# First and last layer of a four-layer graph network: float16 products accumulated in one 256-column half of a bank, four output banks in turn

## The reference

```python
# layer 0
node_att = softmax(x @ node_w, axis=0)
h = x @ edge_w
e = where(adj > 0, h @ h.T, NEG_BIG)
output = adj * (node_att * softmax(e, axis=1)) @ (x @ weight) + bias
# layer 1: gated sum of an attention with rank-one scores and of adj @ (x @ W_gcnb)
# layer 2: relu(normalised (adj + I) @ (x @ weight))
# layer 3
h = relu(adj @ (x @ W1) + b1)
h = relu(adj @ (h @ W2) + b2)
output = adj @ (h @ W3) + b3
# after each layer: x = layernorm(x + output)
```

## Time and profile before

| | |
|---|---|
| median of 3 runs | 790.58 us (789.51 to 792.78) |
| the profiled execution | 791.85 us, its span 790.0 us |
| granted TensorE clock over the span | 0.988 of full speed |
| PE busy | 744.8 us (94%), 4192 matmuls |
| DVE busy | 452.6 us (57%) |
| ACT, POOL busy | 347.4 us, 120.0 us |
| `weighted`, L696 and L698 | 256 and 256 matmuls |
| last product, L953 and L963 | 64 and 192 matmuls |
| layer 0's rounds | about 46 to 213 us of the span |
| last product | 726.8 us to the end |

### The profile page before, as it was taken

One profiled execution on the slowest core, in us unless ns is written; L12 is line 12 of the kernel. 1 busy time (PEld: TensorE's weight loads), 2 busy tenths in 40 slices (PEclk: granted clock), 3 DMA queues, 4 the chain that ended last, 5 costly groups with the idle time before them and its releaser, 6 DMA issues.

```text
span 790.0 us, 11567 instructions
## 1 busy us (share of the span) xinstructions
PE 744.8 (94%) x4192; PEld 489.8 (62%) x4192; DVE 452.6 (57%) x934; ACT 347.4 (44%) x530; POOL 120.0 (15%) x246
## 2 busy tenths in 40 slices
PE   7888999797999999999989999999999999999997
PEld 6776766564678878787835545675664546465343
DVE  4485888688768797988944475121271311114465
ACT  4678877675385474646722243132270322224000
POOL 2011222111321012111122340000001000000343
PEclk9998999998999999999999999999999999999999
DMA  8948889996568509400030000000000000000011
GB/s 230 180 91 146 162 164 159 167 155 112 103 95 153 88 2 159 68 2 1 1 87 1 0 0 1 1 0 0 0 0 27 1 1 0 0 0 0 21 41 46
DMA packets 114300, 48.71 MB, mean 62 GB/s; under 512 B 103504, under 2 KB 109776, under 8 KB 114256
## 3 DMA queue, kind: packets, MB, share of 16 engines
q1 hardware_dynamic: 110224, 33.44, 21.7%
q0 software_dynamic: 4032, 14.68, 11.2%
HBM read 35.53 MB, written 2.10 MB: 48 GB/s over the span
## 4 chain that ended last, share of the span: by engine, by line
PE 43%; DVE 7%; issue 3%; ACT 1%; POOL 1%; DVEq 0%; POOLq 0%; ACTq 0%
PE ps L777 11%; PE ps L928 11%; PE ps L904 8%; PE ps L963 4%; PE ps L937 3%; PE ps L887 3%; PE ps L953 2%; DVE stats L1297 1%; PE ps L633 1%; DVE es_lo L1285 1%; DVE x L1575 1%; DVE tm L1495 1%; DVE agg_lo L1483 1%; DVE y L1619 0%; DVE y L1697 0%
## 5 line engine op out<-in xcount | busy, mean ns | idle before, releaser
L777 PE MATMUL ps<-adjT,x 128*128 128x512 bf16 (+1 forms) x768 | 173.3, 379 | 5.1 <-DVE agg_lo L1483 2.5
L777 PEld LDWEIGHTS ps<-adjT,x 128*128 128x128 f16 x768 | 72.3, 98 | 90.4 <-issue 7.6
L696 PE MATMUL ps<-sup,turned 128*128 128x512 f16 x256 | 88.3, 393 | 12.1 <-DVE y L1350 12.1
L1285 DVE TENSOR_TENSOR hh_lo<-hf,hh_hi 128x512 fp32r<-128x512 f32 x32 | 22.2, 693 | 134.5 <-ACT hf L1221 133.5
L928 PE MATMUL ps<-adjT,G 128*128 x384 | 83.6, 379 | 0.4 <-ACT hf L1221 0.4
L819 PE MATMUL ps<-H_hi,es_hi 128*128 128x258 f32 x256 | 76.8, 300 | 2.2 <-DVE es_lo L1285 1.7
L819 PE MATMUL ps<-H_lo,es_hi 128*128 128x258 f32 x256 | 72.4, 283 | 0.0
L819 PE MATMUL ps<-H_hi,es_lo 128*128 128x258 f32 x256 | 72.4, 283 | 0.0
L698 PE MATMUL ps<-sup,turned 128*128 128x256 f16 x256 | 71.7, 280 | 0.0
L928 PEld LDWEIGHTS ps<-adjT,G 128*128 128x128 f16 x384 | 37.3, 98 | 45.4 <-issue 0.9
L492 POOL TENSOR_TENSOR rstd<-mv,epsc 128x1 f32<-128x1 f32 x64 | 15.2, 238 | 295.9 <-DVE mv L1299 295.9
(11 more groups left out here) (216 smaller groups left out, 1484.7 us busy)
## 6 DMA issues: line engine op xcount, KB each, us to landing
adjb<-in_adj POOLq DMA_DIRECT2D x16, 512.0 KB, 7.0
adjf<-in_adj POOLq DMA_DIRECT2D x12, 512.0 KB, 6.4
x<-in_x SPq DMA_DIRECT2D x4, 512.0 KB, 6.0
out<-adjf SPq DMA_DIRECT2D x16, 128.0 KB, 1.7
adjf<-in_L_gnn_W SPq DMA_DIRECT2D x1, 1024.0 KB, 5.9
W1f<-in_L_gnn_W SPq DMA_DIRECT2D x1, 512.0 KB, 3.7
adjf<-in_L_gnn_W SPq DMA_DIRECT2D x1, 512.0 KB, 3.9
we<-in_L_gnn_edge_w SPq DMA_DIRECT2D x1, 256.0 KB, 3.8
```

What stands on the lines that cost most here:

```text
L696: ins = mm(bank(6 + u), PT(HI, t)[:, jt, :], sup[:, jt, :], start=(jt == 0), stop=False, skip_group_check=True)
L777: ins = mm(bank(4 + f), x16[:, part, jt, f * P:(f + 1) * P], adj(b, jt), start=(jt == 0 and part == HI), stop=(jt == T - 1 and part == LO))
L1285: return tt(to, frm, high.bitcast(F32), ALU.subtract)
```

## The change

Both products now accumulate all their parts in the same 256 columns, in matmuls of 256 columns. In layer 0 three of them (P_hi S_hi, P_hi S_lo, P_lo S_hi) stand where one of 512 and one of 256 stood; in the last product two stand where one of 512 stood. The number of columns streamed is the same; each matmul brings its weight load. DVE reads 256 columns once (L1350 and L1699 are gone, and the semaphore `xb_used` with them). The last product takes banks 0 to 3 in turn, so a tile waits for the read of tile t - 4, and tiles 4 to 7 wait for nothing. DVE's register loop over the last tiles is written out.

```diff
-                    ins = mm(bank(6 + u), PT(HI, t)[:, jt, :], sup[:, jt, :], start=(jt == 0), stop=False,
-                             skip_group_check=True)
-                    ins = mm(bank(6 + u, D), PT(LO, t)[:, jt, :], sup[:, jt, 0:D], start=False, stop=(jt == T - 1),
-                             skip_group_check=True)
+                    for part, c0 in ((HI, 0), (HI, D), (LO, 0)):
+                        ins = mm(bank(6 + u, D), PT(part, t)[:, jt, :], sup[:, jt, c0:c0 + D],
+                                 start=(jt == 0 and (part, c0) == (HI, 0)), stop=(jt == T - 1 and part == LO))
...
-                    ins = mm(bank(4 + k), adjT[:, 0, jt, k * P:(k + 1) * P], f16[:, jt, :], start=(i == 0),
-                             stop=(i == T - 1))
+                    for part in (HI, LO):
+                        ins = mm(bank(4 + k, D), adjT[:, 0, jt, k * P:(k + 1) * P], f16[:, jt, part * D:part * D + D],
+                                 start=(i == 0 and part == HI), stop=(i == T - 1 and part == LO))
...
             def out3(b, k):
-                t, u = TB * b + k, k % 2
-                if not (isinstance(b, int) and k < 2):
-                    pe.wait_ge(o3_read, t - 1)
+
+                if not isinstance(b, int):
+                    pe.wait_ge(o3_read, TB * b + k - TB + 1)
                 for jt in range(T):
-                    ins = mm(bank(u), adjT[:, bass.ds(b, 1), jt, k * P:(k + 1) * P].rearrange("p a c -> p (a c)"),
-                             f16[:, jt, :], start=(jt == 0), stop=(jt == T - 1))
+                    for part in (HI, LO):
+                        ins = mm(bank(k, D), adjT[:, bass.ds(b, 1), jt, k * P:(k + 1) * P].rearrange("p a c -> p (a c)"),
+                                 f16[:, jt, part * D:part * D + D], start=(jt == 0 and part == HI),
+                                 stop=(jt == T - 1 and part == LO))
...
-                stt(y[:, u, :], bank(6 + u, D), rowf[:, u, 2:3], xb[:, u, :], ALU.mult, ALU.add).then_inc(xb_used, 1)
-                dve.wait_ge(xb_used, t + 1)
-                stt(y[:, u, :], ps[:, 6 + u, D:2 * D], rowf[:, u, 2:3], y[:, u, :], ALU.mult, ALU.add) \
-                    .then_inc(pv_read, 1)
+                stt(y[:, u, :], bank(6 + u, D), rowf[:, u, 2:3], xb[:, u, :], ALU.mult, ALU.add).then_inc(pv_read, 1)
...
             def final3(t, u):
-                at = 4 + t if isinstance(t, int) and t < TB else u
+                at = 4 + t if t < TB else t % TB
...
-                stt(y[:, u, :], bank(at, D), g1[:, 3:4], xb[:, u, :], ALU.mult, ALU.add).then_inc(xb_used, 1)
-                dve.wait_ge(xb_used, T + t + 1)
-                stt(y[:, u, :], ps[:, at, D:2 * D], g1[:, 3:4], y[:, u, :], ALU.mult, ALU.add).then_inc(o3_read, 1)
+                stt(y[:, u, :], bank(at, D), g1[:, 3:4], xb[:, u, :], ALU.mult, ALU.add).then_inc(o3_read, 1)
...
-            pair3(1)
-            with dve.Fori(2, T // 2) as i:
-                own.enter(i - 2, 2)
+            for i in range(1, T // 2):
                 pair3(i)
-            own.leave(T // 2 - 2)
```

More of the change, by code:

```diff
@@ L357, in build @@
         PT_landed = [sem(f"PT_landed{part}") for part in (HI, LO)]
-        pv_mm, pv_read, xb_ready, xb_used = sem("pv_mm"), sem("pv_read"), sem("xb_ready"), sem("xb_used")
+        pv_mm, pv_read, xb_ready = sem("pv_mm"), sem("pv_read"), sem("xb_ready")
         y_normed = sem("y_normed")
@@ L494, in norm_factor, with bias_x @@
                     .then_inc(rstd_ready, 1)
-            def bias_x(t, u, before=0):
-                wait_from(pool, xb_used, before + t - 1)
+            def bias_x(t, u, used):
+                wait_from(pool, used, t - 1)
                 nc.gpsimd.tensor_tensor(xb[:, u, :], tile(x, t), brow[:, :], ALU.add).then_inc(xb_ready, 1)
@@ L522, in _ @@
                 load_adj(t)
-            bias_x(0, 0)
-            bias_x(1, 1)
+            bias_x(0, 0, pv_read)
+            bias_x(1, 1, pv_read)
             def load_later(t):
@@ L544, in _ @@
                 if t + 2 < T:
-                    bias_x(t + 2, t % 2)
+                    bias_x(t + 2, t % 2, pv_read)
                 if t + 2 * AB < T:
@@ L610, in _ @@
             nc.gpsimd.partition_all_reduce(g1[:, 1:2], g1[:, 0:1], P, RMAX).then_inc(gmax_ready, 1)
-            bias_x(0, 0, T)
-            bias_x(1, 1, T)
+            bias_x(0, 0, o3_read)
+            bias_x(1, 1, o3_read)
             with pool.Fori(0, T // 2 - 1) as i:
@@ L617, in _ @@
                     norm_factor(3 * T + 2 * i + u, u)
-                    bias_x(2 * i + 2 + u, u, T)
+                    bias_x(2 * i + 2 + u, u, o3_read)
             own.leave(T // 2 - 1)
```

## The result

| | before | changed |
|---|---|---|
| median of 7 runs | 792.78 us | 786.98 us |
| lowest to highest | 789.51 to 794.17 | 783.11 to 806.39 |
| ratio, 95% interval | | 0.9919 (0.9891 to 0.9948) |
| profiled execution: time, span | 791.85, 790.0 | 785.21, 783.4 |

A second measurement of the same two kernels, 12 and 17 runs on another chip (the last experiment), gave 787.99 and 791.14 us, ratio 0.9963 (0.9939 to 0.9987). The kernel is faster by 0.4 to 0.8%; the predicted time of 785.6 was 1.4 us too low by the first median and 2.4 by the second, and the range of 782.5 to 790.5 held both. Two of the first seven runs, at 802 and 806 us, lie far above the others.

The account below looks back on a forecast made before the run. PE bounds the kernel at both ends of layer 0 and in the last product, DVE with near-full DMA queues between. Layer 0's -2.9 and the last product's -2.1 us take 790.58 to 785.6 us; range 782.5 to 790.5.

Parts of the forecast that it names:

- The last product: Last product and tail: wait gone -2.1 us, one read less in the tail -0.52, pace +0.5; sum -2.1 us.
- The pace: Last product: 256-column matmuls start 0.109 us apart, their loads costing nothing; +0.5 us over 256 pairs.
- The two ends of layer 0: Layer 0, 79 to 125 us and from 202 us: PE full, shorter reads give nothing; `weighted` rows cost +0.1 and +0.07 us.
- 125 to 153 us: Layer 0 with full DMA engines: one read's gain, 0.52 us, gets through; bounds 0 and 0.52 for each of four reads.
- nothing swallowed: Rival, layer 0: the DMA queues swallow none of the gain; 783.5 us, chance 0.07.
- The rival by which all of layer 0's gain is swallowed: Layer 0: the DMA queues swallow the whole gain, only the last product gains; 788.7 us, chance 0.17.
- 153 to 202 us: Layer 0 after the loads, DVE the bound: five reads of 0.52 plus 0.52 let through start `weighted(14)` 3.1 us earlier.
- The fifth read: Layer 0, 153 to 202 us: it lies inside DVE's 1.42 us wait for a transpose at 196.75, so its gain is swallowed.
- The step that failed: Layer 0, 196.75 us: the awaited transpose, issued by DVE's own P_lo, moves with it, so four earlier reads count.
- the rival on code fetches: DVE's issue waits in layer 1 move onto or off the path: 788 us with one more, 783 with one less; chance 0.13.
- The sum: Whole kernel: layer 0 -2.9 us and last product -2.1, together -5.0, passed on through the untouched layers between.

Follow-up runs that it names:

- e3: Kernel before, with four banks in turn and DVE's loop written out in the last product, still 512 columns and two reads: 789.42 us, ratio 0.998.
- e4: Changed kernel, with two banks in turn in the last product in place of four: 791.49 us, ratio 0.9968.
- e2: Kernel before, with only the last product changed (256-column matmuls, single read, four banks): 789.99 us, ratio 0.9983.
- e8: Changed kernel, with each matmul of the last product cut in two, to 128 columns: 786.41 us in one run.
- e1: Changed kernel, with the last product put back as before, so only layer 0 is changed: 788.46 us, ratio 0.9964.
- e5: Changed kernel, with a second DVE pass over the same bank in layer 0, its result overwritten: 789.94 us, ratio 0.9964.
- e7: Kernel before, with one further adjacency row loaded in round 9 of layer 0 in place of round 5: 789.21 us, ratio 0.9974.
- e6: Changed kernel, with one further adjacency row loaded in round 9 of layer 0 in place of round 5: 785.24 us, ratio 0.9905.

## Why the prediction was right, and where it was off

**The last product**, -2.1 us, came out to 0.2 us in the profile: 63.2 to 61.3. The pace is (42.08 - 0.27) / 383 = 0.109 us, as taken, with the loads under it. No new wait came with four banks. That the wait had two independent causes, and that either edit alone removes it (e3, e4), the prediction had not said.

**The two ends of layer 0** held: PE was full in both, and the last two rows gave back 0.08 us (4.65 ahead at `weighted(14)`, 213.03 - 208.46 = 4.57 at the last matmul) where 0.07 were forecast.

**125 to 153 us** was put at one read let through, 0.52 us, of four. The profile shows 152.18 - 151.37 = 0.81, and 1.23 counted from `weighted(1)`, which started 0.42 later in this execution. That does not settle the term, since profiles of the same layer 0 differ by more. From `weighted(1)` to this multiplication they take 72.9, 74.3 and 76.6 us with two reads (before, e3, e2) and 71.7, 72.1 and 72.9 with one (changed, e8, e1). On the mean that is 2.4 us, nearer to "nothing swallowed" than to the forecast, but the two groups touch. The rival by which all of layer 0's gain is swallowed falls by the rounds behind the stretch. The wait itself took another form: before, DVE waited 3.81 us for its own transpose; now ACT waits 6.2 for the transpose of P_hi and DVE 4.13, which the profile puts down to issue (that it is for ACT is my reading), and 0.32 for its own. DVE's waits together grew by 0.64.

**153 to 202 us** was -3.1 us at `weighted(14)` and measured -4.65: 0.81 from the stretch ahead, 2.10 from four reads (2.08 forecast), 0.52 from the last as forecast, and 1.22 that the sum did not have. The fifth read was to lie inside the wait and be swallowed, and it does. From `negm` at 188.00 to the multiplication at 196.75 it was 8.75 us before; from 185.09 to 192.62 it is 7.53 now, and 7.54 in e5, where the second read is back and DVE waits 0.26 for the transpose in place of 0.72. The step that failed is that this transpose *"is issued by DVE's own P_lo and so moves with it"*. Its issue moves so, 2.51 us behind `negm` in all three, but its time from issue to landing, which the sum left as it was, fell from 6.2 to 5.0 us. Issues over just that stretch, before and after (190.5 to 196.7 and 187.6 to 192.6 us; queue: packets, MB, share; issues: median us to landing):

```profile
q8 instruction: 1, 0.02, 1.0%
q14 instruction: 1, 0.01, 0.4%
...
turned<-pl SPq DMA_TRANSPOSE x1, 6.2
adjT<-adjf SPq DMA_TRANSPOSE x1, 5.5
```

```profile
q14 instruction: 1, 0.01, 0.4%
...
turned<-pl SPq DMA_TRANSPOSE x1, 5.0
adjT<-adjf SPq DMA_TRANSPOSE x1, 4.6
```

Before, a second fetch of code, on q8, falls into it. In all four profiles with layer 0's old matmuls (before, e2, e3, e7) the fetch is there, the transpose lands after 6.1 to 6.2 us and DVE waits 1.3 to 1.4 us; in all ten with the new ones it is not, the transpose lands after 5.0, and DVE waits 0.7, or 0.3 in e5 with its second read. So something like the rival on code fetches came with the forecast, as a gain of 1.2 us in layer 0 and not in DVE's waits of layer 1. No run moves the fetch alone: the earlier landing comes with the short matmuls of layer 0 (e1 and e5 have it, e2 and e3 do not), but that they bring it by moving the fetch is not shown.

**The sum.** -4.70 at the first matmul of the last product, against -2.9, and -1.93 behind it: -6.6 us in the profiled execution, against -5.0. The medians came out at -5.8 us in the first measurement and -3.2 in the second. Executions at 794 to 810 us are mixed in, a term that the prediction did not have; without the long ones the medians differ by 6.1 and 4.3. So the forecast of -5.0 lies between the two measurements partly by luck: it missed 1.2 us of gain in layer 0 and a loss by long executions, and these are of opposite sign. Its 785.6 us also started from the 790.58 of three runs, which became 792.78 with seven. The prediction asked what a shorter round of DVE releases earlier, and named the transposes; POOL's load, which is released by DVE's variance in the same round, moves ahead as well, up to the P_hi transpose.

## What to carry to other kernels

When an engine off the bound gets faster, list every queue whose issues it releases, and how they come to stand against each other, not only their sum: here one semaphore wait that keeps a bulk load behind the two transposes of its row was worth 4.2 us on the chip on which the change itself was worth 3.2. Before a wait is credited to one edit of several, ask which of them would remove it alone. And where the waiting is for a transfer, take its time from issue to landing as a term of its own.

## What the runs showed of the hardware

- Float16 matmuls with a load each pace at 0.216, 0.109 and 0.056 us for 512, 256 and 128 columns; loads of 98 ns were hidden in all three (at 128 columns three of four loads repeated the weights).
- A load of 512 KB and a DMA transpose issued about 0.3 us apart can drop the DMA engines to 50 GB/s at a DMA share of 1.3 to 1.4 for some 20 us, and don't always. With the load behind the transposes it was in none of 16 executions.
- In the same stretch PE's granted clock fell to 0.81 in e6, from 113 to 122 us, so a part of that stretch was at 1.2 GHz; PE had been busy 6.17 of the 9 us before. In the changed kernel's profile PE had no gap from 79 to 125 us and its clock stayed at 1.00, 2.4 GHz.
- A 16 KB fetch of code beside a transpose went with a landing 1.2 us later (6.2 us after issue against 5.0), in 4 of 4 profiles against 0 of 10; that it is the cause is not shown.
